# Ternary feed-forward networks: fp32 products in place of split float32r pairs

## The chip, the cores and the metric

The kernel runs on one core of one Trainium2 chip. The metric is the device time of one execution in microseconds (us). Its engines run side by side and are tied by semaphores: TensorE (PE, matrix products into PSUM), VectorE (DVE), ScalarE (ACT), GpSimd (POOL), and SyncE (SP), which issues most DMAs. A wait in the code is `wait_ge(semaphore, value)`; `.then_inc` raises a semaphore when an instruction is done.

## The reference

One sequence of 2048 tokens with 128 features passes through eight residual steps, each on the layer-normalized input: gated linear attention (GLA), a ternary feed-forward network, a state-space layer (SSM), the same ternary network again, a top-k sparse attention with latent keys, an int8 gated network, a linear attention, and the int8 network again.

```python
def _L0_ffn_ref(x, w1_w, w1_s, w2_w, w2_s, h1_w, h1_s, h2_w, h2_s, w3_w, w3_s):
    def _tlin(x, w, s):
        return jnp.einsum('bsi,oi->bso', x, w) * s
    h = jax.nn.silu(_tlin(x, w1_w, w1_s)) * _tlin(x, w2_w, w2_s)
    h = jax.nn.gelu(_tlin(h, h1_w, h1_s), approximate=False)
    h = jax.nn.gelu(_tlin(h, h2_w, h2_s), approximate=False)
    return _tlin(h, w3_w, w3_s)
x = x + _L0_attn_a_ref(_layernorm(x), ...)
x = x + _L0_ffn_ref(_layernorm(x), ...)
x = x + _L0_attn_b_ref(_layernorm(x), ...)
x = x + _L0_ffn_ref(_layernorm(x), ...)
...
```

The weights w1, w2 (512 x 128), h1, h2 (512 x 512) and w3 (128 x 512) hold only -1, 0 and 1, stored as fp32; each output has a scale.

## The kernel before

**Layout.** Features lie on the 128 partitions, tokens along the free axis. The sequence is worked in four chunks of C = 512 tokens; a half is two chunks. One PSUM bank holds 128 x 512 fp32, and there are eight.

**Stages.** GLA goes over 16 tiles of 128 tokens. Then the function `ffn_half(R)` of each engine runs for R = 0 to 3: the two halves of the first network, then the two halves of the second; norms and the SSM of the same halves are written in between (L1095 to L1118). Then `topk_front`, `topk` (136 slots, one for each group of 16 queries and a few at the ends, filled by a planner's costs), and the last stages. The order on each engine is that of the program; nothing is reordered but by the semaphores.

**A half of a network.** Up: steps j = 0 to 7 (two chunks, four blocks of 128 hidden rows), each a product on w1 and one on w2 into two of banks 0 to 3; ACT takes SiLU of the one (L1679), DVE multiplies by the other (L2194). Hidden: steps q = 0 to 15 (two layers, two chunks, four blocks), each four accumulated products into bank q % 4 and a GELU on ACT (L1706). Down: four accumulated products on w3 for each chunk, added to x by DVE (L2242).

**How a product is split.** float32r is a rounded form of fp32. The kernel keeps every activation as a rounded copy (hi) and a float32r remainder (lo) and multiplies both by the weights, rounded once: two matmuls for each product. POOL makes the rounded copies (`x_round` L761, L769, L777) and DVE the remainders (`x_rest` L2173, `gated_rest` L2185, L2210). ACT and DVE write the unsplit value to a ring of four tiles, f_full, so ACT waits until the remainder four steps back has been read (L1703, L1705). POOL casts the five weight tiles during GLA (L728); PE waits for them before R = 0 (L1535), and so does SP before it loads the merged attention weights (L619), which land where the unrounded weights were.

**The gathers.** In the attention stage POOL issues 496 indirect DMAs (`gather_rows`, L791), 32 a tile (16 for tile 0), each filling one row on every partition of a buffer; two buffers alternate, and from tile 2 on a gather waits until PE has used the rows of two tiles before (L803). The first five of tile 0 stand inside `ffn_half(3)` (L783). SP copies the fixed rows of tile 0 after the last down product (L676 to L680).

## Time and profile before

| | us |
|---|---|
| median of three runs | 1074.12 |
| the runs | 1074.12, 1074.72, 1063.49 |
| span of the profiled execution | 1068.8 |
| busy: PE, DVE, ACT, POOL | 941.6, 786.1, 692.7, 583.4 |
| the two networks with the SSM between them, 134.9 to 354.6 | 219.7 |
| front of the attention stage, to 385.3 | 30.7 |
| attention stage, to 987.8 | 602.5 |
| last stages, to 1068.8 | 81.0 |

The profile names no other time of the profiled execution than its span, which runs from its first to its last instruction. Times of the trace are counted from the start of the span. A fp32 matmul shows as two records of one product, a float32r one as one. The end of a matmul record is modelled and overlaps the next, so the distance between starts tells how fast PE issues. "Idle" in a row stands before the instruction, with what ended it.

### The profile page before, as it was taken

The numbers are of one execution on the slowest core, as the hardware profiler recorded it, in microseconds if no ns is written. First come the engines' busy times: TensorE is split into PE (matmuls) and PEld (weight loads), VectorE is DVE, ScalarE is ACT, GpSimd is POOL, SyncE is SP. The second block draws the span as 40 slices with busy tenths as digits, with TensorE's granted clock in tenths as the row PEclk, the third lists the DMA queues.
The fourth block names the chain that finished last, engine by engine and source line by source line (L and its number), as shares of the span: only waits on it lengthen the run. The fifth ranks groups of instructions, "written<-read, shape, count | busy, mean of one in ns | idle before, by whom it ended". The sixth has DMA issues, their size and how long they took to land. (4 is left out here: it accounts for less than half of the span.)

```text
span 1068.8 us, 19776 instructions
## 1 busy us (share of the span) xinstructions
PE 941.6 (88%) x6850; PEld 690.5 (65%) x6850; DVE 786.1 (74%) x1468; ACT 692.7 (65%) x1920; POOL 583.4 (55%) x622
## 2 busy tenths in 40 slices
PE   8999999999999977787889988888988897897786
PEld 5888868676767336556656666666767676576544
DVE  4888875757466788987895898797698979733346
ACT  5767655555564476694695678786687776656454
POOL 0111044333333777777777667777777777776001
PEclk9999999999999678997795689897798978989899
DMA  7100001000000563533522423331331333131001
GB/s 237 40 21 2 2 1 45 1 1 1 1 1 12 124 146 92 132 81 80 130 59 61 101 61 73 73 70 41 73 73 38 73 73 74 47 105 40 1 1 39
DMA packets 58737, 62.07 MB, mean 58 GB/s; under 512 B 27760, under 2 KB 43152, under 8 KB 58256
## 3 DMA queue, kind: packets, MB, share of 16 engines
q1 hardware_dynamic: 42768, 36.41, 13.2%
q0 software_dynamic: 15872, 24.41, 10.1%
q8 instruction: 55, 0.90, 0.3%
q14 instruction: 42, 0.34, 0.1%
HBM read 52.65 MB, written 8.13 MB: 57 GB/s over the span
## 5 line engine op out<-in xcount | busy, mean ns | idle before, releaser
L791 POOL DMA_INDIRECT gathered_rows<-key_table,idx_T x496 | 482.5, 973 | 157.6 <-issue 146.6
L2382 DVE TENSOR_TENSOR turned_rows<-bank,rank_rope 96x512 f32<-96x512 f32 x128 | 87.3, 682 | 83.3 <-PE bank L1293 82.1
L1293 PE MATMUL bank<-ident,gathered_rows 128*96 128x128 f32 x512 | 92.6, 311 | 11.8 <-DVE turned_rows L2382 7.1
L2356 DVE SCALAR_TENSOR_TENSOR index_sums<-index_relu,iw,index_sums 128x512 f32<-128x512 f32 (+4 forms) x114 | 75.4, 661 | 33.4 <-ACT index_relu L1826 30.8
L832 PE MATMUL bank<-index_k_hi,index_q 128*128 128x512 f32 (+5 forms) x160 | 77.2, 485 | 19.3 <-DVE idx_T L2376 11.6
L1826 ACT ACTIVATE index_relu<-bank 128x512 f32<-128x512 f32 (+4 forms) x152 | 75.1, 507 | 24.0 <-PE bank L832 23.6
L1848 ACT ACTIVATE probs<-masked_scores,attn_columns 128x208 f32<-128x208 f32 x128 | 59.5, 465 | 31.3 <-DVE attn_columns L2392 26.7
L832 PE MATMUL bank<-probs_window,local_values 80*32 80x128 f32 x256 | 57.4, 311 | 24.7 <-ACT probs_picked L1864 23.1
L1293 PEld LDWEIGHTS bank<-ident,gathered_rows 128*96 128x96 f32 x512 | 66.0, 144 | 20.5 <-issue 11.4
L2364 DVE MAX8 top<-index_sums 128x8 f32<-128x320 f32 (+13 forms) x56 | 75.8, 1354 | 1.0
L2366 DVE FIND_INDEX8 idx_u<-top,index_sums 128x8 uint32<-128x320 f32 (+13 forms) x56 | 75.5, 1348 | 0.0
L1872 ACT ACTIVATE attn_out<-bank 32x128 f32<-32x128 f32 x128 | 32.6, 255 | 64.5 <-PE bank L832 64.4
L832 PE MATMUL bank<-keys_and_latents,q_window 96*128 96x80 f32 x256 | 52.4, 291 | 17.0 <-DVE x L2399 17.0
L832 PE MATMUL bank<-index_k_lo,index_q 128*128 128x512 f32 (+5 forms) x160 | 63.6, 401 | 0.0
L1857 ACT ACTIVATE probs<-probs,attn_columns 128x208 f32<-128x208 f32 x128 | 59.9, 468 | 4.2
L832 PE MATMUL bank<-turned_rows,q_picked 96*32 96x128 f32 x1024 | 61.8, 318 | 0.0
L832 PEld LDWEIGHTS bank<-probs_picked,gathered_rows 128*32 128x32 f32 x1024 | 59.7, 123 | 2.1
L832 PEld LDWEIGHTS bank<-keys_and_latents,q_window 96*128 96x128 f32 x256 | 46.0, 225 | 21.7 <-DVE turned_rows L2382 21.4
L832 PE MATMUL bank<-probs_picked,gathered_rows 128*32 128x32 f32 x1024 | 59.1, 206 | 0.0
L1317 PE MATMUL bank<-ident,probs 128*128 128x128 f32 x128 | 41.5, 324 | 17.1 <-ACT probs L1857 15.5
L1317 PEld LDWEIGHTS bank<-ident,probs 128*128 128x128 f32 x128 | 19.8, 154 | 56.5 <-ACT probs L1857 37.7
L2368 DVE MATCH_REPLACE8 index_sums<-top,index_sums 128x320 f32<-128x320 f32 (+13 forms) x42 | 56.3, 1339 | 0.0
(295 smaller groups left out, 2430.4 us busy)
## 6 DMA issues: line engine op xcount, KB each, us to landing
queries_in<-q_rot SPq DMA_DIRECT2D x32, 256.0 KB
gathered_rows<-key_table,idx_T POOLq DMA_INDIRECT x496, 2.5
q_rot<-rotated SPq DMA_DIRECT2D x16, 256.0 KB, 3.3
queries_in<-q_lat SPq DMA_DIRECT2D x16, 256.0 KB
h<-in_h SPq DMA_DIRECT2D x2, 1024.0 KB, 7.9
q_lat<-q_latent_sb SPq DMA_DIRECT2D x8, 256.0 KB
local_values<-key_table SPq DMA_DIRECT2D x15, 80.0 KB
rope_tables<-in_cos_ql SPq DMA_DIRECT2D x4, 256.0 KB
```

The lines of the kernel that those rows point to most:

```text
L791: pool.indirect_dma_start(out=G[i % 2][:, gather_place(i, q), :], out_offset=None, in_=key_table[0:index_width(i), :], in_offset=bass.Indi ...
L832: return pe.matmul(out_, lhsT, rhs, start=start, stop=stop, **kw)
L1293: last = pe.transpose(bank[2][0:ROW, j * P:(j + 1) * P], G[i % 2][:, gather_place(i, 4 * g + j), :], ident[:])
L1317: pe.transpose(score_bank(n)[:, 0:P], Pr[n % 2][:, 0:P], ident[:])
L1826: fn(r_, bank[6 + u % 2][:, 0:w], ACT.Relu).then_inc(i_relu, 1)
L1848: fn(Pr[n % 2], Sm[n % 2], ACT.Exp, scale=-1.0, bias=least[:, n % 2:n % 2 + 1], accum_out=ssum[:, n % 2:n % 2 + 1]).then_inc(a_exp_s, 1)
L1857: fn(Pr[n % 2], Pr[n % 2], ACT.Copy, scale=rsum[:, n % 2:n % 2 + 1]).then_inc(a_pn, 1)
L2356: v.scalar_tensor_tensor(s_, r_, iw[:, h:h + 1], s_, ALU.mult, ALU.add).then_inc(i_used, 1)
L2364: steps.did(v.max(best, sc))
L2366: steps.did(v.max_index(idx_u[:, 8 * k:8 * k + 8], best, sc))
L2368: steps.did(v.match_replace(sc, best, sc, TAKEN))
L2382: v.tensor_tensor(GT[n % 2].rearrange("r (j p) -> r j p", j=4), bank[2][0:ROW, :].rearrange("r (j p) -> r j p", j=4), rank_rope[:].unsquee ...
```

## The change

Both networks multiply the fp32 activation by the fp32 weight in one product. POOL's rounded copies, DVE's remainders, POOL's weight casts and the seven semaphores for them are gone. The weights are loaded directly to where their rounded copies were. Gated values, first and second GELU have a buffer each (f_a, f_b, f_c), so the waits on the ring are gone. PE waits for the norm itself (`ln_applied`) before the up steps, and for the GELU or the gated value before hidden and down steps. SP no longer waits for the casts, nor for the last down product before the fixed rows, whose place in the arena is free now. POOL issues all gathers of tile 0 in `gather(0)`, with no wait for the up products. Outside the diff everything is the same; the last stages still split their operands.

```diff
--- before.py
+++ after.py
@@ -171,8 +171,8 @@
         lam, log_dt, sBT, sCT, sD = (load(n) for n in ("lam", "log_dt", "sBT", "sCT", "sD"))
 
         early_offset = (nc.sbuf_base + 31) // 32 * 32
-        h1, h2, w1, w2, w3, Wgk1, Wgk2 = (load(n) for n in ("h1", "h2", "w1", "w2", "w3", "Wgk1", "Wgk2"))
-        early_rest = sb("early_rest", [P, 2 * P])
+        early_rest = sb("early_rest", [P, 3 * T - 2 * P])
+        Wgk1, Wgk2 = load("Wgk1"), load("Wgk2")
         assert nc.sbuf_base - early_offset == 4 * 3 * T
         w1s, w2s, h1s, h2s, w3s = (load(n) for n in ("w1s", "w2s", "h1s", "h2s", "w3s"))
         Wkeys, Wdq, Wqr1, Wqr2 = (load(n) for n in ("Wkeys", "Wdq", "Wqr1", "Wqr2"))
@@ -227,17 +227,23 @@
         S, S_in = [part(P) for _ in range(2)], part(P)
 
         at[0] = ARENA_LO
-        w1r, w2r, w3r = over("w1r", [HID], F32R), over("w2r", [HID], F32R), over("w3r", [NM, P], F32R)
-        h1r, h2r = over("h1r", [NM, HID], F32R), over("h2r", [NM, HID], F32R)
+        for n, shape in (("w1", [HID]), ("w2", [HID]), ("w3", [NM, P]), ("h1", [NM, HID]), ("h2", [NM, HID])):
+            LOAD[n] = over(n, shape)
+        w1, w2, w3, h1, h2 = (LOAD[n] for n in ("w1", "w2", "w3", "h1", "h2"))
         GATE_AT = at[0] - ARENA_LO
         gate = part(T)
         oT = gate
         at[0] = LAYER
 
-        x_hi, x_lo = (over("ffn_x_" + n, [2, C], F32R) for n in ("hi", "lo"))
-        a_hi, a_lo = (over("ffn_a_" + n, [2 * NM, C], F32R) for n in ("hi", "lo"))
-        b_hi, b_lo = (over("ffn_b_" + n, [2 * NM, C], F32R) for n in ("hi", "lo"))
-        SILU_AT = at[0]
+        x_hi, x_lo = (over("last_x_" + n, [2, C], F32R) for n in ("hi", "lo"))
+        LAST_AT = at[0]
+        at[0] = LAYER + P // QD * ROW
+        f_a, f_c, f_b = (over("ffn_" + n, [2 * NM, C]) for n in ("gated", "second", "first"))
+        SILU_AT = LAYER + 36 * C
+        at[0] = LAST_AT
+        a_hi, a_lo = (over("last_a_" + n, [2 * NM2, C], F32R) for n in ("hi", "lo"))
+        assert at[0] <= SILU_AT
+        at[0] = SILU_AT
         f_silu_sb, f_full = over("ffn_silu_out", [2, C]), over("ffn_full", [4, C])
 
         a_exp, a_dt, a_neg, a_dec = (over("ssm_" + n, [8], parts=64)[:, 0:1] for n in
@@ -388,10 +394,8 @@
                 "read_out", "read_out_copied", "out_gate_projected", "out_gate_copied", "out_gate_sigmoid", "out_gate",
                 "squared", "mean_sq", "rms", "rms_columns", "rms_turned", "normed", "projected_out"))
 
-        (f_w, f_x_hi, f_x, f_up, f_silu, f_gated, f_gated_hi, f_a, f_hid, f_gelu, f_gelu_hi, f_lo, f_down) = (
-            sem("ffn_" + n) for n in (
-                "weights_rounded", "x_hi", "x_split", "up", "silu", "gated", "gated_hi", "gated_split", "hidden",
-                "gelu", "gelu_hi", "gelu_split", "down"))
+        f_up, f_silu, f_gated, f_hid, f_gelu, f_down = (
+            sem("ffn_" + n) for n in ("up", "silu", "gated", "hidden", "gelu", "down"))
 
         ss_a, ss_u, ss_x, ss_y = (sem("ssm_" + n) for n in ("decay_ready", "inputs", "states", "outputs"))
 
@@ -616,7 +620,6 @@
                 sp.dma_start(dst[:], d[n]).then_inc(s_int, 16)
 
 
-            sp.wait_ge(f_w, 5)
             for n, dst in (("WuqT", WuqT), ("WukT", WukT), ("WuvT", WuvT), ("Wout", Wout)):
                 sp.dma_start(dst, d[n]).then_inc(t_w, 16)
 
@@ -673,7 +676,6 @@
             load_key_rope(0)
             store_rows(0)
             sp.wait_ge(t_store_k, STORES_K)
-            sp.wait_ge(f_down, 8)
             for tq in range(QD):
                 sp.dma_start(G[0][tq * JG:(tq + 1) * JG, gather_place(0, 0):gather_place(0, 0) + FIXED // QD, :],
                              key_table[LW:KTOP, :].unsqueeze(1).to_broadcast([JG, FIXED // QD, ROW]))\
@@ -722,11 +724,6 @@
 
             def gla():
 
-                def round_weights(tile, *pairs):
-                    pool.wait_ge(g_G, tile + 2)
-                    for dst, src in pairs:
-                        pool.tensor_copy(dst[:], src[:]).then_inc(f_w, 1)
-
                 def out_gate(c):
                     pool.wait_ge(g_gs, c + 1)
                     if c:
@@ -734,15 +731,9 @@
                     pool.tensor_tensor(chunk(gate, c), chunk(gate, c), og_sig, ALU.mult).then_inc(g_gate, 1)
 
                 out_gate(0)
-                pool.wait_ge(s_ffn, N_FFN)
-                round_weights(2, (w1r, w1), (w2r, w2))
-                round_weights(3, (h1r, h1))
                 for i in range(NT):
                     if SVC_ACT.get(i, ("", 0))[0] == "gate":
                         out_gate(SVC_ACT[i][1])
-                    if i == 2:
-                        round_weights(5, (h2r, h2))
-                        round_weights(6, (w3r, w3))
                     if i == 6:
                         pool.wait_ge(s_int, 48)
                         pool.wait_ge(g_G, 11)
@@ -751,41 +742,6 @@
 
             gla()
 
-            def x_round(R, which=(0, 1)):
-
-                k, r = HALVES[R]
-                for u in which:
-                    pool.wait_ge(ln_applied, LN0 + norm_index(k, r) + u + 1)
-                    if R > 0:
-                        pool.wait_ge(f_up, 8 * R)
-                    pool.tensor_copy(x_hi[:, u, :], xn[:, (2 * r + u) * C:(2 * r + u + 1) * C]).then_inc(f_x_hi, 1)
-
-            def ffn_half(R):
-
-                for j in range(2 * NM):
-                    pool.wait_ge(f_gated, 8 * R + j + 1)
-                    if R > 0 and j % NM == 0:
-                        pool.wait_ge(f_down, 2 * R - 1 + j // NM)
-                    pool.tensor_copy(a_hi[:, j, :], f_full[:, j % 4, :]).then_inc(f_gated_hi, 1)
-                for q in range(4 * NM):
-                    stage, u, m = q // 8, q // 4 % 2, q % 4
-                    pool.wait_ge(f_gelu, 16 * R + q + 1)
-                    if stage == 0 and R > 0 and m == 0:
-                        pool.wait_ge(f_hid, 16 * R)
-                    if stage == 1 and m == 0:
-                        pool.wait_ge(f_hid, 16 * R + 4 * u + 4)
-                    pool.tensor_copy((b_hi, a_hi)[stage][:, u * NM + m, :], f_full[:, q % 4, :]).then_inc(f_gelu_hi, 1)
-                    if R == 3 and q >= EARLY_GATHER:
-                        if q == EARLY_GATHER:
-                            pool.wait_ge(t_store_k, STORES_K)
-                            pool.wait_ge(f_up, 32)
-                            pool.wait_ge(i_idx, 1)
-                        gather_rows(0, FIXED // QD + q - EARLY_GATHER)
-                    if q == 10 and R < 3:
-                        x_round(R + 1)
-
-            EARLY_GATHER = 11
-
             def gather_rows(i, q):
 
                 pool.indirect_dma_start(
@@ -796,16 +752,14 @@
             def gather(i):
 
                 pool.wait_ge(i_idx, i + 1)
+                if i == 0:
+                    pool.wait_ge(t_store_k, STORES_K)
                 if i == 1:
                     pool.wait_ge(f_hid, 64)
-                for q in range(FIXED // QD + 4 * NM - EARLY_GATHER if i == 0 else 0, P // QD):
+                for q in range(FIXED // QD if i == 0 else 0, P // QD):
                     if i >= 2 and q % (GQ // QD) == 0:
                         pool.wait_ge(a_pv, NG * (i - 2) + q // (GQ // QD) + 1)
                     gather_rows(i, q)
-
-            x_round(0)
-            for R in range(4):
-                ffn_half(R)
 
             for i in range(NT):
                 if i >= 4 and i % 4 == 0:
@@ -1034,24 +988,22 @@
 
             def ffn_up(R, j):
 
-                u, m = divmod(j, NM)
+                (k, r), (u, m) = HALVES[R], divmod(j, NM)
                 if m == 0:
-                    pe.wait_ge(f_x, 2 * R + u + 1)
+                    pe.wait_ge(ln_applied, LN0 + norm_index(k, r) + u + 1)
                 if j >= 2:
                     pe.wait_ge(f_gated, 8 * R + j - 1)
                 elif R > 0:
                     pe.wait_ge(f_gelu, 16 * R - 2 + 2 * j)
-                for o_, w in ((bank[2 * (j % 2)], w1r), (bank[2 * (j % 2) + 1], w2r)):
-                    mm(o_, w[:, m * P:m * P + P], x_hi[:, u, :], True, False)
-                    last = mm(o_, w[:, m * P:m * P + P], x_lo[:, u, :], False, True)
+                for o_, w in ((bank[2 * (j % 2)], w1), (bank[2 * (j % 2) + 1], w2)):
+                    last = mm(o_, w[:, m * P:m * P + P], chunk(xn, 2 * r + u))
                 last.then_inc(f_up, 1)
 
             def ffn_down(R, u):
 
                 for kk in range(NM):
-                    pe.wait_ge(f_lo, 16 * R + 8 + u * NM + kk + 1)
-                    mm(bank[6 + u], w3r[:, kk, :], a_hi[:, u * NM + kk, :], kk == 0, False)
-                    last = mm(bank[6 + u], w3r[:, kk, :], a_lo[:, u * NM + kk, :], False, kk == NM - 1)
+                    pe.wait_ge(f_gelu, 16 * R + 8 + u * NM + kk + 1)
+                    last = mm(bank[6 + u], w3[:, kk, :], f_c[:, u * NM + kk, :], kk == 0, kk == NM - 1)
                 last.then_inc(f_down, 1)
 
             def ffn_half(R):
@@ -1078,19 +1030,17 @@
                         norm_var(*FIRST_NORM[R])
                 for q in range(4 * NM):
                     stage, u, m = q // 8, q // 4 % 2, q % 4
-                    w, hi, lo = ((h1r, a_hi, a_lo), (h2r, b_hi, b_lo))[stage]
+                    w, from_ = ((h1, f_a), (h2, f_b))[stage]
                     if q < 4:
                         pe.wait_ge(f_gated, 8 * R + 7 + m // 2)
                     else:
                         pe.wait_ge(f_gelu, 16 * R + q - 3)
                     for kk in range(NM):
                         if m == 0 and stage == 0:
-                            pe.wait_ge(f_a, 8 * R + u * NM + kk + 1)
+                            pe.wait_ge(f_gated, 8 * R + u * NM + kk + 1)
                         elif m == 0:
-                            pe.wait_ge(f_lo, 16 * R + u * NM + kk + 1)
-                        wt = w[:, kk, m * P:m * P + P]
-                        mm(bank[m], wt, hi[:, u * NM + kk, :], kk == 0, False)
-                        last = mm(bank[m], wt, lo[:, u * NM + kk, :], False, kk == NM - 1)
+                            pe.wait_ge(f_gelu, 16 * R + u * NM + kk + 1)
+                        last = mm(bank[m], w[:, kk, m * P:m * P + P], from_[:, u * NM + kk, :], kk == 0, kk == NM - 1)
                     last.then_inc(f_hid, 1)
                     if R == 0:
                         if q == 0:
@@ -1532,7 +1482,7 @@
                 down(NCH - 1)
 
             gla()
-            pe.wait_ge(f_w, 5)
+            pe.wait_ge(s_ffn, N_FFN)
             for R in range(4):
                 ffn_half(R)
             topk_front()
@@ -1699,11 +1649,7 @@
                 for q in range(4 * NM):
                     m, sc = q % 4, (h1s, h2s)[q // 8]
                     act.wait_ge(f_hid, 16 * R + q + 1)
-                    if q >= 4:
-                        act.wait_ge(f_lo, 16 * R + q - 3)
-                    else:
-                        act.wait_ge(f_a, 8 * R + 5 + m)
-                    fn(f_full[:, q % 4, :], bank[m], ACT.Gelu, scale=sc[:, m:m + 1]).then_inc(f_gelu, 1)
+                    fn((f_b, f_c)[q // 8][:, q % 8, :], bank[m], ACT.Gelu, scale=sc[:, m:m + 1]).then_inc(f_gelu, 1)
                     if R == 3:
                         early_setup(q)
                     if R == 0:
@@ -2154,10 +2100,6 @@
                 cumulate(1)
                 for i in range(NT):
                     tile(i, i % 2)
-                    if i == 12:
-                        dve.wait_ge(s_ffn, N_FFN)
-                        x_rest(0, (0,))
-                x_rest(0, (1,))
                 gla_read_out(NT - 1)
 
             def norm_apply(k, r, which=(0, 1)):
@@ -2165,12 +2107,6 @@
                     dve.wait_ge(ln_sd, norm_index(k, r) + u + 1)
                     own = chunk(xn, 2 * r + u)
                     v.tensor_tensor(own, bank[4 + u], own, ALU.mult).then_inc(ln_applied, 1)
-
-            def x_rest(R, which=(0, 1)):
-                for u in which:
-                    c = 2 * (R % 2) + u
-                    dve.wait_ge(f_x_hi, 2 * R + u + 1)
-                    v.tensor_tensor(x_lo[:, u, :], chunk(xn, c), x_hi[:, u, :], ALU.subtract).then_inc(f_x, 1)
 
             def merge_weights():
                 dve.wait_ge(t_wm, GH + 1)
@@ -2180,24 +2116,13 @@
                         .then_inc(t_wc, 1)
 
             def ffn_half(R):
-                def gated_rest(j):
-                    dve.wait_ge(f_gated_hi, 8 * R + j + 1)
-                    v.tensor_tensor(a_lo[:, j, :], f_full[:, j % 4, :], a_hi[:, j, :], ALU.subtract).then_inc(f_a, 1)
-
                 for j in range(2 * NM):
                     m = j % NM
                     dve.wait_ge(f_silu, 8 * R + j + 1)
-                    if j >= 4:
-                        dve.wait_ge(f_a, 8 * R + j - 3)
-                    elif R > 0:
-                        dve.wait_ge(f_lo, 16 * R)
-                    v.scalar_tensor_tensor(f_full[:, j % 4, :], bank[2 * (j % 2) + 1], w2s[:, m:m + 1],
+                    v.scalar_tensor_tensor(f_a[:, j, :], bank[2 * (j % 2) + 1], w2s[:, m:m + 1],
                                            f_silu_sb[:, j % 2, :], ALU.mult, ALU.mult).then_inc(f_gated, 1)
-                    if j >= 1:
-                        gated_rest(j - 1)
                     if R > 0 and j == 1:
                         add_down(R - 1, 1)
-                gated_rest(2 * NM - 1)
                 norm_apply(*FIRST_NORM[R], which=(0,) if R == 0 else (0, 1))
                 if R == 0:
                     ssm_decay()
@@ -2205,9 +2130,6 @@
                     dve.wait_ge(s_tk, N_TK)
                     piece_end(0, PIECES.index("raw"))
                 for q in range(4 * NM):
-                    hi, lo = ((b_hi, b_lo), (a_hi, a_lo))[q // 8]
-                    dve.wait_ge(f_gelu_hi, 16 * R + q + 1)
-                    v.tensor_tensor(lo[:, q % 8, :], f_full[:, q % 4, :], hi[:, q % 8, :], ALU.subtract).then_inc(f_lo, 1)
                     if R in (1, 2):
                         c0 = 2 * (R - 1)
                         if q in (1, 2):
@@ -2230,8 +2152,6 @@
                         merge_weights()
                     if R == 3:
                         early_setup(q)
-                    if q == 10 and R < 3:
-                        x_rest(R + 1)
                 add_down(R, 0)
                 if R == 3:
                     add_down(R, 1)
```

## Rows read from the trace of the kernel before

**Rows 1.** The page's first line: the span.
```profile
span 1068.8 us, 19776 instructions
```
**Rows 2.** Busy time by stretch: start:end, length, busy PE, PEld, DVE, ACT, POOL (count), clock, DMA, GB/s.
```profile
0.00:134.90 134.90, 131.09 (x1514) 106.98 (x1514) 107.63 (x215) 89.53 (x178) 13.50 (x17) 0.99 0.20 60
134.90:354.60 219.70, 211.28 (x868) 150.79 (x856) 141.37 (x230) 118.93 (x178) 89.35 (x110) 1.00 0.03 8
353.40:370.60 17.20, 17.14 (x28) 6.22 (x29) 11.82 (x20) 7.37 (x12) 13.10 (x14) 0.50 0.58 123
354.60:385.30 30.70, 25.86 (x57) 10.46 (x57) 22.07 (x41) 18.88 (x34) 23.39 (x25) 0.72 0.79 184
385.30:987.80 602.50, 510.71 (x4172) 383.40 (x4170) 478.02 (x919) 426.16 (x1447) 452.13 (x466) 0.84 0.32 75
```
**Rows 3.** Products by form, PE, 134.9 to 354.6: count, busy, mean ns, idle before.
```profile
L832 PE MATMUL bank<-ffn_a_hi,h1r 128*128 128x512 f32 x128 | 55.7, 435 | 0.0
L832 PE MATMUL bank<-ffn_x_hi,w1r 128*128 128x512 f32 x32 | 15.1, 471 | 4.6 <-DVE ffn_full L2194 3.6 <-DVE arena_hi L2054 0.8
L832 PE MATMUL bank<-ffn_a_hi,w3r 128*128 128x512 f32 x32 | 13.0, 408 | 1.9 <-DVE ffn_a_lo L2210 1.9
L832 PE MATMUL bank<-x,center 128*128 128x512 f32 x24 | 12.0, 601 | 0.2
L832 PE MATMUL bank<-xn,ones 128*128 128x512 f32 x24 | 11.4, 592 | 0.0
```
**Rows 4.** Timeline of PE in half R = 3: start, us, what.
```profile
313.26 0.39 PE L832 MATMUL bank<-ffn_a_hi,h1r 128*128 128x512 f32 x1
313.49 0.40 PE L832 MATMUL bank<-ffn_a_lo,h1r 128*128 128x512 f32 x1
313.72 1.02 PE L832 MATMUL bank<-xn,Wik 128*128 128x512 f32 x2
314.58 1.02 PE L832 MATMUL bank<-xn,Wiq 128*128 128x512 f32 x2
```
**Rows 5.** Timeline of ACT, up steps of half R = 0.
```profile
142.28 0.69 ACT L1679 ACTIVATE ffn_silu_out<-bank,w1s 128x512 f32<-128x512 f32 x1 [0.63 <-PE bank L832]
...
145.04 0.69 ACT L1679 ACTIVATE ffn_silu_out<-bank,w1s 128x512 f32<-128x512 f32 x1 [0.63 <-PE bank L832]
```
**Rows 6.** Timeline of SP's DMA queue.
```profile
354.78 1.94 SPq L678 DMA_DIRECT2D gathered_rows<-key_table  x4
```
**Rows 7.** Timeline of DVE around the end of half R = 3.
```profile
340.83 0.19 DVE L2376 CAST idx_T<-bank 128x32 uint32<-128x32 f32 x1
...
358.73 0.19 DVE L2376 CAST idx_T<-bank 128x32 uint32<-128x32 f32 x1 [3.25 <-PE bank L832]
358.83 0.68 DVE L2283 SCALAR_TENSOR_TENSOR mu<-bank,mu 128x512 f32<-128x512 f32 x1
...
368.95 0.69 DVE L2304 TENSOR_TENSOR rotated<-ln_diag 128x512 f32<-128x512 f32 x1
```
**Rows 8.** Timeline of POOL: first gather, first of tile 1, one that waited.
```profile
342.58 1.51 POOL L791 DMA_INDIRECT gathered_rows<-key_table,idx_T  x1 [0.23 <-issue]
...
366.65 1.03 POOL L791 DMA_INDIRECT gathered_rows<-key_table,idx_T  x1 [0.30 <-issue]
...
620.40 0.95 POOL L791 DMA_INDIRECT gathered_rows<-key_table,idx_T  x1 [2.58 <-PE bank L832]
621.65 0.94 POOL L791 DMA_INDIRECT gathered_rows<-key_table,idx_T  x1 [0.30 <-issue]
```
**Rows 9.** The tile gathered_rows over the whole span: us and times of idling before its instructions.
```profile
  PE bank L832: 11.0, 16
  DMA gathered_rows<-key_table,idx_T: 10.1, 6
```
**Rows 10.** Timeline of PE at the end of half R = 3.
```profile
351.19 0.40 PE L832 MATMUL bank<-ffn_a_lo,w3r 128*128 128x512 f32 x1
353.46 0.80 PE L832 MATMUL bank<-ffn_a_hi,w3r 128*128 128x512 f32 x1 [1.88 <-DVE ffn_a_lo L2210]
```

## The prediction

> **What bounds the kernel now.** I read the span first, then the busy time by stage, then inside the feed-forward stage the matrix products by form and one by one, then what releases the engines at its end, and last the gathers of the attention stage, because the change ends before that stage but moves its start.
>
> The profiled execution spans 1068.8 us [rows 1]; the page gives it no other time, and the median of the runs, 1074.1, lies 5.3 above it. I sum against the span and add 5.
>
> The stages [rows 2]: the two networks run from the first product on w1r at 134.9 to the last down product at 354.6, 219.7 us. TensorE (PE) is busy in 211.3 of them at the full clock (1.00 in that row, the 2.4 GHz level); VectorE (DVE) in 141.4, ScalarE (ACT) in 118.9, GpSimd (POOL) in 89.4. PE sits idle 8.4 us in all. So this stage is bound by PE, and the work that the change removes from DVE and POOL lies beside it. The attention stage, 385.3 to 987.8, is the long one: PE 511 of 602 us and a chain of gathers on POOL.
>
> **The price of a product.** The changed code issues, per half of the sequence, 8 up steps of 2 products, 16 hidden steps of 4 and 2 down steps of 4, so 16 + 64 + 8 = 88, and 352 for the four halves. Today each is a pair, rounded copy and remainder; the forms show it (128 records of ffn_a_hi on h1r, 32 on w1r, 32 on w3r, and so on) [rows 3]. Issue times are what counts, not the mean duration of a record, which overlaps the next. From one 128x512 float32r matmul to the next it is 313.49 - 313.26 = 0.23 us [rows 4]; in undisturbed stretches of the same view 0.227, so 0.454 a pair. Plain fp32 products stand in the same stage, under the same clock: the index key product takes two records and the next begins 314.58 - 313.72 = 0.86 us later [rows 4]; I use 0.857. Nothing in that row depends on what the numbers are, so ternary weights get no discount.
>
> The Trainium skill, page "FP8 and Floating Point Precision", section "TensorE Precision Notes", says that true fp32 takes four passes through the array. By that and the float32r row as one pass a product would be an estimated 0.91 us and the term below 160 instead of 142; the row has 0.857, and the measured price stays in the sum.
>
> **The change, part by part.**
>
> First, **the products**: 352 x (0.857 - 0.454) = +141.9 us on PE, if PE lost no waiting. The number of PE records does not change (two per pair, two per fp32 product).
>
> Second, **the waiting that goes**. Of the 219.7 us, 352 x 0.454 = 159.8 are pairs; the forms list 40 other 128x512 fp32 products (two records each; x,center 24 and xn,ones 24 are the largest [rows 3]), 34.3 us. The rest, 25.6, is small products (turns, merged weights, early index scores, some 7 us by my count of their records) and waiting. The floor of the waiting is the idle 8.4 [rows 2], of which 3.6 was for the gated product on DVE and 1.9 for the last remainder [rows 3]; the ceiling is about 18.6. How the up steps wait: two up steps are 145.04 - 142.28 = 2.76 us apart [rows 5], and PE issues 1.82 of it; the other 0.94 is the ACT and DVE round trip, through two pairs of PSUM banks. The loop is one step's issue (0.91) plus 1.85 of latency. With fp32 it is 1.71 + 1.85 = 3.56, against 3.43 that PE issues itself: 0.07 a step, on 24 steps 1.7 us. The hidden steps wait for a bank four steps back, 3.4 us each then, while the whole ACT chain of a norm with two table loads is about 5; hidden. The early index scores' waits (ACT, 1 to 2 us) and a start-up us stay. So some 5 us of waiting remain, and 13 go, nearer to the middle of floor and ceiling than to either: -13 (bounds 0 if new waits replace them all, -18.6).
>
> Third, **what leaves DVE, POOL and ACT**: 104 casts and 104 subtractions, five weight casts, and the waits of ACT and DVE on them. DVE is at 64% of the stage and POOL at 41% [rows 2], so this is worth nothing beyond the waiting already counted. In the GLA stage two subtractions and the casts go; PE is busy 131.1 of 134.9 there [rows 2]: -0.5, bounds 0 and -1.
>
> Fourth, **loads and queues**. The weights land straight in the arena by the same copies; PE first needs them at 134.9, and the merged-weight loads on SP's queue no longer wait for the casts: they move forward some 40 us into a stretch where the early loads are done. Cost 0. SP's wait for f_down before the fixed-row copies is gone; they were issued at 354.78 [rows 6] and now follow the key-row store inside the stage. They left the DMA queues where the share is 0.79 [rows 2]: 0, bounds -1 and 0.
>
> Fifth, **gathers on POOL**. The first five of tile 0 sat between casts; the index rows were ready at 340.83 [rows 7], the first gather began at 342.58 and tile 1's at 366.65 [rows 8]. Now 16 gathers at 621.65 - 620.40 = 1.25 us [rows 8] take 20 us from that index on, under the last five hidden steps and the downs (5 x 3.43 + 6.9 = 24 us). Tile 1's then wait for its indices, which came at 358.73, 4.1 after the stage's end [rows 7]: POOL gains about 8 us of lead on the readers. I cost that at nothing: at 620.40 POOL waited 2.58 us for a product that frees its buffer [rows 8], 11.0 us over 16 such waits [rows 9]. A larger lead is lost in those waits. If that cover failed, the gain could be at most the 10.1 us that PE waits for gathers [rows 9].
>
> Sixth, **the front of the attention stage**. Between 353.4 and 370.6 the granted clock is 0.50 (the 1.2 GHz level) with PE busy 17.14 of 17.2 [rows 2]; before it fell PE had idled 1.88 us for the last remainder [rows 10], a wait the change removes. At full clock the same PE work would take 8.6 less. But DVE is next: its pieces and rotations run from 358.83 to 369.6 almost without a gap [rows 7], and only the first query product, which releases ACT, moves them earlier by about 1 us. I take -1.5, bounds 0 and -8.6.
>
> Sum: 1068.8 + 141.9 - 13 - 0.5 - 1.5 = 1195.7, plus 5: **1200 us**.
>
> **The rivals.**
> A. No waiting is won back: new bank waits (a step's products finish late for ACT, whose table loads then lie bare) replace the old. For it: the up loop stays a hair longer than PE's own issue. Against it: in the hidden steps ACT has 3.4 us for a 0.7 us GELU. 1200 + 13 = 1213. Chance 0.13.
> B. The attention stage gives time back: PE stays at the full clock through the front, and the gather lead survives to the tail. 1200 - (8.6 - 1.5) - 10.1 = 1183. For it: PE has no gap left before the front; against it: DVE's row of work and the 16 buffer waits. The Trainium skill, page "TensorE: Matmul & The Clock Gate", section on the clock gate, says that the clock is set by how busy the engine has been; by that rule the stretch would run at full clock, which is the first half of this case, and the rows agree only in that the fall follows an idle gap. Chance 0.20.
> C. The other side: the product does not cost what its neighbours cost, for instance because two passes suffice for these operands, and the two records are as short as float32r's. Place: the 352 products. The stage after is 352p + 46.9 us, so it breaks even at p = 0.49; at p = 0.454 the result is 1068.8 - 15 + 5 = 1059. Against it: every fp32 form of 512 columns in this trace has the long records. Chance 0.02.
> D. The attention stage itself falls into another pattern of half clock: its row has 0.84, so about a third of 602 us ran at half; a shift of its start by 130 us could move that by 10 to 20 us either way. Chance 0.05.
> The forecast keeps 0.60, its own range 1189 to 1209.
>
> **How the numbers follow.** The range holds the forecast and most of A and B: 1182 to 1218. About 1% is what can be told from no change here (the runs lie within 1063 and 1075); faster 0.02 (C), within 1% 0.01, slower 0.97.
>
> **What would show it.** Right: in the stage 352 fp32 products starting 0.857 apart, its length 219.7 + 129 = 349 us; PE busy above 97% in it; DVE about 71 us less busy; up steps 1.75 to 1.80 apart; the attention stage within 5 us of its 602.5; more POOL waits for PE than 11 us. Wrong: a product at another price (step one); a stage of 360 or more (step two, A); a front below 25 us instead of 30.7, or gathers no longer waited for at the end (five and six, B); an attention stage that differs by over 10 us (D).

## The result, and the profile after

The kernel after takes **1200.4 us** in the median of four runs (1192.75 to 1202.84), the kernel before 1073.7 in four runs (1063.49 to 1074.72). The ratio is 1.119, 95% interval 1.114 to 1.125. The forecast was 1200, range 1182 to 1218.

The profiled execution of the kernel after took 1198.94 us and spans 1197.1. The page's first lines answer to [rows 1]:

```profile
span 1197.1 us, 19437 instructions
...
PE 1076.4 (90%) x6850; PEld 694.6 (58%) x6850; DVE 712.6 (60%) x1364; ACT 694.4 (58%) x1920; POOL 493.2 (41%) x513
```

The same view as [rows 2], by stretch, of the kernel after. The first row is the feed-forward stage, the next three are the front of the attention stage, the attention stage and the end; the fifth is the front up to the first fall of the clock in it. The same stretch of before ran at 0.50 (the row 353.4 to 370.6).

```profile
134.90:484.40 349.50, 348.01 (x873) 152.74 (x861) 68.02 (x127) 120.53 (x178) 15.28 (x16) 1.00 0.04 9
484.40:512.40 28.00, 19.62 (x57) 8.86 (x57) 22.05 (x41) 18.70 (x34) 19.50 (x20) 0.91 0.65 160
512.40:1115.00 602.60, 513.74 (x4173) 385.95 (x4172) 478.31 (x919) 426.57 (x1447) 446.71 (x461) 0.83 0.34 75
1115.00:1197.10 82.10, 63.93 (x254) 39.98 (x254) 36.93 (x65) 38.97 (x84) 5.00 (x6) 0.89 0.04 13
...
484.40:500.60 16.20, 11.78 (x34) 4.62 (x34) 12.41 (x20) 10.53 (x18) 10.58 (x10) 1.00 0.44 108
```

Set beside [rows 2], the whole difference of the spans, 128.3 us, is placed: the feed-forward stage +129.8 (349.5 against 219.7), the front -2.7 (28.0 against 30.7), the attention stage +0.1, the end +1.1 (82.1 against 81.0); both stages begin at 134.9. In the feed-forward stage DVE is 73 us less busy and POOL 74, PE 137 us more, and PE is busy in 99.6% of it. What the change saves on DVE and POOL lies, but for some 12 us of PE's waiting (below), where nobody waits; all that it costs lies on the engine that is the bound.

The products by form, answering to [rows 3] (count, busy, mean ns, idle before):

```profile
L786 PE MATMUL bank<-ffn_gated,h 128*128 128x512 f32 x256 | 113.8, 595 | 0.0
L786 PE MATMUL bank<-ffn_first,h 128*128 128x512 f32 x256 | 111.8, 594 | 0.0
L786 PE MATMUL bank<-xn,w 128*128 128x512 f32 x128 | 58.1, 599 | 0.0
L786 PE MATMUL bank<-ffn_second,w 128*128 128x512 f32 x64 | 28.6, 592 | 0.0
```

That is 704 records, two for each of 352 products, with no idle time before any form. Mean record: about 595 ns, where those of the split products in [rows 3] had 408 to 471. The price is in the starts. The timeline of PE at the end of the last half (it groups neighbours: x18 is nine products):

```profile
469.68 7.89 PE L786 MATMUL bank<-ffn_first,h 128*128 128x512 f32 x18
477.40 7.03 PE L786 MATMUL bank<-ffn_second,w 128*128 128x512 f32 x16
484.36 1.98 PE L786 MATMUL bank<-cq,Wqr 64*128 64x512 f32 x4
```

Nine products of the second hidden layer take 477.40 - 469.68 = 7.72 us, 0.858 each (the price taken from [rows 4] was 0.857); the eight down products take 6.96, 0.87 each. Then PE goes on to the query product without the 1.88 us of [rows 10].

The up steps on ACT, answering to [rows 5]:

```profile
143.21 0.69 ACT L1629 ACTIVATE ffn_silu_out<-bank,w1s 128x512 f32<-128x512 f32 x1 [1.92 <-PE bank L786]
...
146.75 0.69 ACT L1629 ACTIVATE ffn_silu_out<-bank,w1s 128x512 f32<-128x512 f32 x1 [1.14 <-PE bank L786]
```

Two steps take 3.54 us, where 3.56 was worked out from 2.76 and the two prices.

DVE's row of work in the front, answering to [rows 7]:

```profile
487.57 0.69 DVE L2203 SCALAR_TENSOR_TENSOR mu<-bank,mu 128x512 f32<-128x512 f32 x1 [0.73 <-ACT mu L1725]
...
497.68 0.69 DVE L2224 TENSOR_TENSOR rotated<-ln_diag 128x512 f32<-128x512 f32 x1
```

And the wait of PE behind that row, from the timeline of PE:

```profile
500.17 1.70 PE L786 MATMUL bank<-xn,Wiq 128*128 128x512 f32 x2 [4.42 <-DVE index_k_lo L2191]
```

From the first to the last of DVE's row it is 10.11 us here and 10.12 before, although PE ran at half clock beside it before and at the full clock now; it starts 3.2 us after the stage's end instead of 4.2. PE does its own part faster and then idles 4.42 us for DVE.

POOL: the first gather, the first of tile 1, and two that waited for a buffer (a pause of 0.30 is the usual one), answering to [rows 8]:

```profile
460.81 1.13 POOL L747 DMA_INDIRECT gathered_rows<-key_table,idx_T  x1 [348.96 <-DVE idx_T L2296]
...
487.11 0.94 POOL L747 DMA_INDIRECT gathered_rows<-key_table,idx_T  x1 [6.45 <-DVE idx_T L2296]
...
531.86 0.94 POOL L747 DMA_INDIRECT gathered_rows<-key_table,idx_T  x1 [3.40 <-PE bank L786]
...
749.44 0.94 POOL L747 DMA_INDIRECT gathered_rows<-key_table,idx_T  x1 [2.57 <-PE bank L786]
```

And all idling before instructions on these buffers, answering to [rows 9]:

```profile
  PE bank L786: 17.9, 15
  DMA gathered_rows<-key_table,idx_T: 11.5, 7
```

Against the start of the attention stage, tile 1's gathers begin 512.4 - 487.1 = 25.3 us ahead; before it was 385.3 - 366.7 = 18.7. POOL gained 6.6 us of lead and waits 17.9 - 11.0 = 6.9 us more for buffers.

### The profile page after: what moved, and what is told of

It reads as the page before. It is cut to its first block and busy times, and to the rows that moved or that the text cites. A ratio compares the mean times of both kernels' runs of the same rounds, so it can differ in the third digit from the quotient of the medians.

```text
span 1197.1 us, 19437 instructions
## 1 busy us (share of the span) xinstructions
PE 1076.4 (90%) x6850; PEld 694.6 (58%) x6850; DVE 712.6 (60%) x1364; ACT 694.4 (58%) x1920; POOL 493.2 (41%) x513
## 5 line engine op out<-in xcount | busy, mean ns | idle before, releaser
L786 PE MATMUL bank<-ffn_gated,h 128*128 128x512 f32 x256 | 113.8, 595 | 0.0
L786 PE MATMUL bank<-ffn_first,h 128*128 128x512 f32 x256 | 111.8, 594 | 0.0
L786 PE MATMUL bank<-index_k_hi,index_q 128*128 128x512 f32 (+5 forms) x160 | 80.1, 503 | 15.1 <-DVE idx_T L2296 7.7
L786 PEld LDWEIGHTS bank<-ffn_gated,h 128*128 128x128 f32 x256 | 48.0, 190 | 62.1 <-issue 59.0
L786 PEld LDWEIGHTS bank<-ffn_first,h 128*128 128x128 f32 x256 | 48.3, 190 | 60.4 <-issue 59.3
L1652 ACT ACTIVATE ffn_second<-bank,h2s 128x512 f32<-128x512 f32 x32 | 22.0, 687 | 83.0 <-PE bank L786 83.0
L1652 ACT ACTIVATE ffn_first<-bank,h1s 128x512 f32<-128x512 f32 x32 | 21.8, 687 | 77.5 <-PE bank L786 77.5
```

The source lines that it names most:

```text
L786: return pe.matmul(out_, lhsT, rhs, start=start, stop=stop, **kw)
L1652: fn((f_b, f_c)[q // 8][:, q % 8, :], bank[m], ACT.Gelu, scale=sc[:, m:m + 1]).then_inc(f_gelu, 1)
```

## The experiments

The theory: 352 products at 0.857 instead of 0.454 us on PE, which is the bound, less about 13 us of PE waiting that goes, partly because a longer product covers more of the round trip over ACT and DVE, partly because no remainder is waited for; the gathers' greater lead and the faster clock in the front are worth next to nothing, since buffers bound the one and DVE the other. The rivals were: another price or new waits that cancel each other; a lead that does pay; an attention stage that moves with its start.

**The price of a product, and what moves behind it.** In `downs_twice` each group of down products of the kernel after is issued twice, with the same operands into the same bank: 32 more fp32 products and no other work.

```diff
-                for kk in range(NM):
-                    pe.wait_ge(f_gelu, 16 * R + 8 + u * NM + kk + 1)
+                for n in range(2 * NM):
+                    kk = n % NM
+                    if n < NM:
+                        pe.wait_ge(f_gelu, 16 * R + 8 + u * NM + kk + 1)
                     last = mm(bank[6 + u], w3[:, kk, :], f_c[:, u * NM + kk, :], kk == 0, kk == NM - 1)
```

> The changed kernel with each group of four down products issued twice into the same bank (the second run of a group starts the bank afresh, so the values are the same). 32 more fp32 products. If the stage of the two networks is bound by TensorE throughout, as the prediction says, they cost 32 x 0.857 = 27.4 us: stage 349.5 + 27.4 = 377, total 1200 + 27 = 1227. If the down products lie beside other work (ScalarE's next table load, the norm), the rival, less than 15 us of it shows: total below 1215.

Measured: 1224.1 us in the median of three runs, 1.142 times the kernel before (1.137 to 1.147). The stage and the attention stage, by stretch:

```profile
134.90:512.00 377.10, 375.61 (x944) 164.97 (x932) 68.21 (x127) 120.59 (x178) 15.32 (x16) 1.00 0.03 8
...
541.30:1142.40 601.10, 513.57 (x4173) 385.28 (x4171) 478.07 (x919) 425.13 (x1441) 448.49 (x460) 0.84 0.33 75
```

The stage grew by 27.6 us, 0.863 for each added product; 32 x 0.857 is 27.4. So an fp32 product costs its issue time in full here; the other bound expected, under 15 us, is out. The attention stage began 29 us later and took 601.1 instead of 602.6, which speaks against rival D. The whole came out 3 us below the 1227 expected; in the profiled execution the attention stage gave 1.5 us and the end 2.4 us back, and the front took 1.3 more.

**The same change for the up steps alone.** `ups_fp32` is the kernel before with only the products on w1 and w2 taken from the fp32 tiles; gated values, hidden and down steps stay split, and the rounded and remainder copies of the input are gone.

```diff
-                    pe.wait_ge(f_x, 2 * R + u + 1)
+                    pe.wait_ge(ln_applied, LN0 + norm_index(*HALVES[R]) + u + 1)
 ...
-                for o_, w in ((bank[2 * (j % 2)], w1r), (bank[2 * (j % 2) + 1], w2r)):
-                    mm(o_, w[:, m * P:m * P + P], x_hi[:, u, :], True, False)
-                    last = mm(o_, w[:, m * P:m * P + P], x_lo[:, u, :], False, True)
+                for o_, w in ((bank[2 * (j % 2)], w1), (bank[2 * (j % 2) + 1], w2)):
+                    last = mm(o_, w[:, m * P:m * P + P], chunk(xn, 2 * HALVES[R][1] + u))
```

> The kernel before with the up products alone in fp32 (their rounded copies and remainders gone, all else as before). TensorE gets 64 x 0.403 = 25.8 us more. My account of the waits: the up loop is one step's issue plus 1.85 us of latency for two steps, 1.38 a step before and 1.78 after, against 0.91 and 1.71 that TensorE issues, so 24 steps x (0.47 - 0.07) = 9.6 us of waiting is won back and the stage grows by 16 (up to 20, where norms already fill the loop): stage about 237, total 1074 + 17 = 1091. Rival 'nothing is won back in the ups, it all comes from the hidden steps and the end': +26, total 1100. Rival 'the up loop is all latency': 32 x 0.4 = +13, total 1087.

Measured: 1088.4 us in the median of four runs, ratio 1.014 (1.010 to 1.018). By that total the forecast of 1091 and the rival at 1087 can't be told apart; the stage tells them apart:

```profile
134.90:373.10 238.20, 234.30 (x879) 151.08 (x868) 137.34 (x223) 119.11 (x178) 81.23 (x103) 1.00 0.02 7
```

It is 18.5 us longer than before, neither 13 nor 26. The 64 products alone would add 64 x 0.403 = 25.8, so the up steps win back 7.3 us of waiting, less than the 9.6 expected. The rest of the change, 129.8 - 18.5 = 111.3 us against 288 x 0.403 = 116.1, wins back 4.8. Together 12.1, where the prediction had 13. Both shares take the price of a product as exact: at the 0.863 of `downs_twice` the products would come to 144.0 and the waiting to 14.2, so the waiting is known to about 2 us. SiLU steps in the timeline of ACT:

```profile
143.36 0.69 ACT L1675 ACTIVATE ffn_silu_out<-bank,w1s 128x512 f32<-128x512 f32 x1 [1.92 <-PE bank L829]
...
146.91 0.69 ACT L1675 ACTIVATE ffn_silu_out<-bank,w1s 128x512 f32<-128x512 f32 x1 [1.15 <-PE bank L829]
```

Two steps take 3.55 us with a split gated value and 3.54 without, so at the fp32 price POOL's and DVE's copies have no part in the pace. In the kernel before they might have: in the up steps of [rows 5] DVE has no idle time, and its two gated values and two remainders fill the 2.76 us:

```profile
144.44 0.75 DVE L2194 SCALAR_TENSOR_TENSOR ffn_full<-bank,w2s,ffn_silu_out 128x512 f32<-128x512 f32 x1
145.11 0.68 DVE L2185 TENSOR_TENSOR ffn_a_lo<-ffn_full,ffn_a_hi 128x512 fp32r<-128x512 f32 x1
145.76 0.75 DVE L2194 SCALAR_TENSOR_TENSOR ffn_full<-bank,w2s,ffn_silu_out 128x512 f32<-128x512 f32 x1
```

`one_rounded` (below) has no remainders and the short product, and its up steps settle it:

```profile
139.40 0.69 ACT L1640 ACTIVATE ffn_silu_out<-bank,w1s 128x512 f32<-128x512 f32 x1 [0.67 <-PE bank L797]
...
141.70 0.69 ACT L1640 ACTIVATE ffn_silu_out<-bank,w1s 128x512 f32<-128x512 f32 x1 [0.61 <-PE bank L797]
```

That is 2.30 us for two steps, and one step's issue of 0.454 plus the same 1.85 of latency is 2.30; with 0.91 it is the 2.76 of before, with 1.71 the 3.56 of after. So one step's issue and the SiLU and gated-value round trip set the pace in all of them, and most of the 7.3 us came back because PE's longer products cover that round trip, not because the copies went.

**The lead of the gathers.** Two kernels take the kernel after and start POOL's gathers later. `late_gathers` holds them until the last half's last hidden step, `later_gathers` until the fourth rotation of the front. Each adds one of the two lines:

```diff
                 if i == 0:
                     pool.wait_ge(t_store_k, STORES_K)
+                    pool.wait_ge(f_hid, 64)     # late_gathers
+                    pool.wait_ge(t_rot, 4)      # later_gathers
```

> The changed kernel, but GpSimd's first gather waits for the last hidden step, so tile 1's gathers begin about 13 us after the stage's end instead of 2.7, as in the kernel before. GpSimd's lead shrinks by about 10 us. Theory: the lead was lost in the waits for a free buffer (17.9 us in the changed kernel), so those shrink to about 8 us and the total stays at 1200, within 3. Rival, the lead is worth its time: total 1208 to 1210.

> The changed kernel, but GpSimd's first gather waits until the queries of chunk 0 are rotated, about 14 us after the stage's end; tile 1's begin 32 us later than in the changed kernel. Theory: the waits for a free buffer (some 13 us net of the usual pause) are used up first and the rest, about 18 us, shows in the end, because the last tiles are read as fast as they are gathered: total 1218. Rival 'the readers set the pace and the lead is never needed': total 1200. Rival 'every microsecond of lead counts': 1232.

Measured: `late_gathers` 1199.3 us (four runs, ratio 1.117, 1.114 to 1.120), level with the kernel after; `later_gathers` 1216.0 (four runs, 1.134, 1.131 to 1.137), 16 us more. Idling before instructions on these buffers in `late_gathers`, from 512 us on (POOL's waits for a buffer, then PE's for data):

```profile
  PE bank L787: 7.6, 11
...
  DMA gathered_rows<-key_table,idx_T: 3.3, 2
```

In `later_gathers`, the same over the whole span (data, then buffers), and the last turn (transposition on PE) of gathered rows in the attention stage:

```profile
  DMA gathered_rows<-key_table,idx_T: 14.9, 10
...
  PE bank L787: 2.4, 8
```

```profile
1132.13 0.64 PE L1244 MATMUL bank<-ident,gathered_rows 128*96 128x128 f32 x4 [1.65 <-DMA gathered_rows<-key_table,idx_T]
```

Tile 1's gathers begin at 499.7 in the first and at 520.2 in the second, 12.6 and 33.1 us later than in the kernel after. The first delay costs nothing that the runs show (the span of its profiled execution is 2.1 us longer, within what runs of one kernel differ by). From the second, the 17.9 - 2.4 = 15.5 us of buffer waits are eaten up, and the rest, 33.1 - 15.5 = 17.6, is close to the 17.2 by which the last turn comes later (1132.1 against 1114.9). In `late_gathers` the buffer waits of the attention stage fall from 17.9 to 7.6, 10.3 us for a delay of 12.6. Taking the usual pause of 0.30 off each wait, the slack is 17.9 - 15 x 0.30 = 13.4 and the rest 19.7. So the buffer waits are the slack of the gathers, read off to within 2 or 3 us, and the lead that the change brought is worth nothing because it adds to a slack that was already there. The first half of that could be read from [rows 8, 9]; only these runs show where it ends. That the slack is small fits the issue times: 496 gathers at 1.25 us are 620 us of POOL's queue, beside an attention stage of 602.6.

**The gap ahead of the front.** In `last_fp32` the very last down product of the kernel before is done in fp32 from the unsplit GELU value, so that PE doesn't wait for its remainder. It costs one product at 0.86 instead of 0.45 us and takes away the 1.88 us of [rows 10], 1.5 us net.

```diff
                 for kk in range(NM):
+                    if R == 3 and u == 1 and kk == NM - 1:
+                        pe.wait_ge(f_gelu, 64)
+                        last = mm(bank[6 + u], w3r[:, kk, :].bitcast(F32), f_full[:, 3, :], False, True)
+                        continue
                     pe.wait_ge(f_lo, 16 * R + 8 + u * NM + kk + 1)
```

> The kernel before with one product changed: the very last down product of the last half takes the unsplit GELU output and the weights in fp32, so it waits for ScalarE only and not for GpSimd's copy and VectorE's remainder. Theory on the front of the attention stage: the 1.88 us gap before the granted clock falls to 0.50 goes, and the same 2.8 us that the changed kernel won in its front (30.7 to 27.9) are won here, with 1.5 us of the gap net of the dearer product: total 4 us under the kernel before, 1069. Rival 'the clock of that stretch does not hang on this gap': 1.5 us or nothing, and the granted clock between 353 and 370 stays 0.50.

Measured: 1066.6 us in the median of 12 runs against 1070.6 in 17 of the kernel before on the same chip, ratio 0.997 (0.994 to 0.9996): 4 us, barely clear of no change. The executions of each kernel spread over 10 to 12 us, and the longer ones are mostly those with the lower mean granted clock (kernel before: 1075.4 us at 0.881, 1066.2 at 0.902). PE at the end of the stage:

```profile
351.19 1.02 PE L832 MATMUL bank<-ffn_full,w3r 128*128 128x512 f32 x2
352.14 1.98 PE L832 MATMUL bank<-cq,Wqr 64*128 64x512 f32 x4
```

By stretch, the stage, the whole front, and the part of it that answers to the half-clocked row of [rows 2]:

```profile
134.90:352.10 217.20, 210.68 (x856) 150.50 (x855) 139.37 (x227) 118.79 (x178) 87.65 (x108) 1.00 0.03 8
...
352.10:380.70 28.60, 21.21 (x57) 9.46 (x57) 23.61 (x45) 18.76 (x34) 21.89 (x23) 0.86 0.86 194
...
353.40:369.30 15.90, 11.55 (x35) 4.57 (x34) 13.65 (x23) 10.72 (x19) 12.24 (x13) 1.00 0.84 180
```

The stage is 2.5 us shorter, 1.0 more than the net gap, since in the kernel before the last pair ran at half clock as well (353.46 to 354.62, 1.16 us instead of 0.45). The front is 2.1 us shorter, and the clock stays full to 369.3. DVE's row in this front:

```profile
355.35 0.69 DVE L2287 SCALAR_TENSOR_TENSOR mu<-bank,mu 128x512 f32<-128x512 f32 x1 [0.23 <-ACT mu L1783]
...
365.46 0.69 DVE L2308 TENSOR_TENSOR rotated<-ln_diag 128x512 f32<-128x512 f32 x1
```

10.11 us once more. By itself this run seems to say that the gap of 1.88 us brought the half clock on. `ups_fp32` contradicts that: it keeps this gap, and its clock stays full. Its last pair of down products, then the stretch that answers to the half-clocked row, and its front:

```profile
372.63 0.50 PE L829 MATMUL bank<-ffn_a_hi,w3r 128*128 128x512 f32 x1 [1.89 <-DVE ffn_a_lo L2202]
```

```profile
371.80:389.00 17.20, 12.05 (x34) 4.66 (x34) 13.32 (x22) 10.53 (x18) 13.19 (x14) 1.00 0.68 157
...
373.10:401.60 28.50, 19.88 (x58) 8.91 (x57) 22.21 (x42) 18.58 (x34) 21.80 (x23) 0.90 0.82 196
```

So a gap of 1.9 us does not by itself bring the clock down, and `last_fp32` does not show that closing it kept the clock up; why it fell in the kernel before stays open. What the clock is worth in the front both runs show, with the gap and without: 28.5 and 28.6 us instead of 30.7. Full clock returns about 2 us of the 8.6 us that PE's own work could give, since DVE sets the pace.

**Half of the work.** `one_rounded` takes the kernel after and makes each of the 352 products a single float32r matmul: ACT and DVE write the activations rounded where they arise, POOL rounds the weights as before, and no remainder is computed, so the activations' precision is that of the rounded form.

```diff
-        f_a, f_c, f_b = (over("ffn_" + n, [2 * NM, C]) for n in ("gated", "second", "first"))
+        f_a, f_c, f_b = (over("ffn_" + n, [2 * NM, C], F32R) for n in ("gated", "second", "first"))
 ...
-                for o_, w in ((bank[2 * (j % 2)], w1), (bank[2 * (j % 2) + 1], w2)):
-                    last = mm(o_, w[:, m * P:m * P + P], chunk(xn, 2 * r + u))
+                for o_, w in ((bank[2 * (j % 2)], w1r), (bank[2 * (j % 2) + 1], w2r)):
+                    last = mm(o_, w[:, m * P:m * P + P], x_hi[:, u, :])
```

> The changed kernel with one float32r product in place of the fp32 one: activations are written rounded by the engine that makes them, no remainder is computed or multiplied (this part of the precision is left out), weights are rounded in GLA as before. TensorE's 352 products cost 0.227 each, 222 us less than in the changed kernel. Theory: TensorE is then no longer the bound; the up loop is (0.91 + 1.85 - 0.45) for two steps, 1.15 a step, and the hidden steps, 0.91 us each of products, wait for ScalarE's table loads, norms and GELUs (120 us busy): stage 160 to 180, total 1010 to 1031. Rival 'the stage stays bound by TensorE': stage 128, total 979.

Measured: 1011.1 us in the median of four runs, ratio 0.944 (0.940 to 0.948). The stage and the front:

```profile
134.90:295.90 161.00, 139.79 (x517) 87.81 (x505) 65.81 (x123) 116.93 (x178) 4.71 (x5) 0.96 0.06 15
295.90:323.90 28.00, 19.69 (x58) 8.97 (x58) 23.52 (x46) 19.07 (x35) 21.29 (x23) 0.92 0.68 168
```

What PE waited for in the stage (us in total, times, longest):

```profile
PE bank L797 <- DVE ffn_gated L2135: 8.1, 11, 1.1
...
PE bank L797 <- ACT ffn_second L1663: 4.8, 2, 3.0
...
PE bank L797 <- ACT ffn_first L1663: 2.7, 2, 2.4
```

PE idles 21.2 us of 161. If the stage were 352 products at 0.227 and the 46.9 us beside them, it would take 126.8; it takes 34 more. Some 21 of them are this idle time; another 7 come from the clock, which stands at 0.50 for 13.6 us of the stage, in four stretches (mean 0.96). Where a product is cheap, the round trips over ACT and DVE come to light, and PE alone no longer bounds the stage. It is the fastest kernel of the study, at lower precision; it shows what the second matmul of each pair cost, not a replacement for either kernel. Of those that keep the full precision, `last_fp32` is the fastest, by the 0.3% said above.

## Why the prediction was right

**The products.** Taken: 352 x 0.403 = 141.9, from [rows 4]. The starts in the kernel after are 0.858 apart, and 32 added ones cost 0.863 each. Held. The cheaper product of rival C does not exist for ternary values: nothing in any record is shorter than in the fp32 forms that were there before.

**The waiting.** Taken: 13 us won back, between 0 and 18.6; measured 141.9 - 129.8 = 12.1. The pace of the up steps was right to 0.02 us. 7.3 of the 12.1 lie in the up steps, where the same working gave 9.6, and 4.8 in the rest, the 1.88 us of the last remainder among them; the sum was nearer than its parts. Only 6.9 of it was visible as idle time of PE in the kernel before (8.4 less the 1.5 that is left); the other 5.2 did not show as idle, presumably because matmul ends are modelled and records overlap. Taking a value between the idle time and the remainder of the stage, not the idle time, was what made this term right; where between was a guess. Rival A (1213) is out: it wanted a stage of 360 us or more, and the stage is 349.5.

**DVE, POOL and ACT, loads and queues.** Costed at nothing, with -0.5 in GLA. DVE and POOL shed 73 and 74 us in the stage, and nothing of it shows in the time beyond the waiting above: the stage takes the same 349.5 us in `late_gathers` and `later_gathers`, where POOL is busy in 4.5 and 0 us of it instead of 15.3. The -0.5 did not appear: the stage starts at 134.9 in both. Nothing speaks of a cost of the moved loads.

**The gathers.** Taken: about 8 us more lead, worth nothing. Measured: 6.6 us more lead, 6.9 us more buffer waits, attention stage +0.1 us. The waits for PE were to exceed 11; they are 17.9. The two late starts show the slack from the other side.

**The front.** Taken: -1.5, bounds 0 and -8.6; measured -2.7. The clock did what rival B's first half said, and most of its time did not follow: PE at full clock between 484.4 and 500.6, and DVE's row 10.11 us long all the same. The reason given for DVE as the bound was right, and so was the 1 us by which its row moves forward; that the work behind the row (index products and the last norm pieces, which need both engines) also gets about 1.7 us quicker was left out. The reason given for the clock, the gap that the change removes, is not shown: in `ups_fp32` the gap is there and the clock stays full. So this part of the term came true without its cause being known. The page "TensorE: Matmul & The Clock Gate" of the Trainium skill, section on the clock gate, has the clock set by how busy the engine has been. The traces agree in part: the clock falls in the kernel after at 500.6, right behind the idle gap of 4.42 us, but the same gap of 1.9 us was followed by 0.50 in the kernel before and by 1.00 in `ups_fp32`.

**The attention stage's pattern** (rival D, -20 to +20). The stage takes 602.6 at a mean clock of 0.83 after a shift of 127 us, against 602.5 at 0.84; 601.1 in `downs_twice`; 601.8, 604.7 and 602.7 in `last_fp32`, `ups_fp32` and `one_rounded`. It moves by at most some 3 us as long as the gathers keep their lead. The end's +1.1 us was in no term, though nothing in it was changed. Its length goes with its granted clock in every kernel: 79.7 us at 0.94 (`downs_twice`), 81.0 at 0.92 (before, `ups_fp32`), 82.1 at 0.89 (after), 83.2 at 0.88 (`last_fp32`) and 84.4 at 0.86 (`one_rounded`). What sets the clock there is open.

**The sum.** 1195.7 was taken for the span and 1197.1 came, from errors of +0.9 (waiting), +0.5 (GLA), -1.2 (front), +0.1 and +1.1. The offset of 5 us between the profiled execution and the median was taken over from the runs of before (1074.1 against 1068.8); here it is 3.3, of which 1.8 is the part of the profiled execution's own time outside its span. So the sum was 1.4 us too low and the offset 1.7 too high. That they cancel, and that the median fell within 0.4 us of the forecast where the four runs lie 10 us apart, is luck; that each large term held is not.

## What to carry to other kernels

Before trading two float32r products for one fp32 product, look for both forms at the same shape in the trace you have and take the distance between their starts: here 0.454 a pair against 0.857, so the "simpler" product costs 1.9 times as much, and work removed from other engines is worth nothing while PE is busy 96% of the stage. Waits for a free buffer on a producer's queue are its slack, within 2 or 3 us here: a gain in its lead only lengthens them, and a delay costs nothing until it has used them up. And an engine at half clock is worth speeding up only as far as the next engine's row of work allows; measure that row in the trace before crediting the clock.

## What the runs showed of the hardware

In the kernel before, an idle gap of 1.88 us on PE was followed by 17.2 us at the half clock in which PE was busy throughout [rows 2, 10]. In `ups_fp32` the same gap, 1.89 us, was followed by 17.2 us at 1.00 with PE busy in 12.05 of them. A gap of 4.42 us at a later place of the kernel after was followed by only 3.4 us at half clock:

```profile
500.60:504.00 3.40, 3.32 (x9) 1.80 (x7) 3.34 (x6) 1.98 (x5) 2.66 (x3) 0.50 0.63 133
```

So the length of one gap set neither whether the clock fell nor how long it stayed down; what does is open. The 17 us at half clock cost some 2 us, since DVE's row of work stood beside them. The end, where 63% of the chain that ended last is PE's (kernel before), was as much as 4.7 us longer at a mean clock of 0.86 than at 0.94, with the same work.
